# Attention with eight of sixteen softmax groups shifted and summed inside the exponential, and the output projection issued behind the next transposes

## The reference, cut to what matters

```python
x = x + _L0_conv_ref(_ln_c(x), rpb_table, w_qkv, w_proj, b_proj)
# inside: 7x7 windows (49 tokens), 4 heads of 32 channels
qkv  = (win @ w_qkv.T)                      # win: (2048, 49, 128)
attn = einsum('bhid,bhjd->bhij', q * scale, k) + bias + mask
attn = softmax(attn, axis=-1)
out  = einsum('bhij,bhjd->bihd', attn, v)
out  = out @ w_proj.T + b_proj
```

## Time and profile before

| What | us |
|---|---|
| median of 3 executions (8311.66 to 8319.39) | 8317.02 |
| the profiled execution's own time | 8316.43 |
| its span, first to last instruction | 8314.5 |
| attention stage, from the start to the last residual | 0 to about 1838 |
| one attention step in the steady part | 6.95 |

### The profile page before, as it was taken

The page is one execution under the profiler, slowest core; times in us unless marked ns, Lnnn a source line. Parts: engine busy times, 40 slices in busy tenths (PEclk is TensorE's granted clock), DMA queues, the critical chain, the costliest instruction groups (busy, mean ns, idle before and its releaser), DMA issues. The chain is left out here.

```text
span 8314.5 us, 428968 instructions
## 1 busy us (share of the span) xinstructions
PE 7686.1 (92%) x164847; PEld 4672.0 (56%) x164847; DVE 6157.6 (74%) x20999; ACT 4825.9 (58%) x15717; POOL 5973.0 (72%) x7343
## 2 busy tenths in 40 slices
PE   7999999978999999988979999979999799999999
PEld 6777777764444444436753333327777555555555
DVE  7999999979999999988856777758888322222222
ACT  4666666655566565558975555536666444444444
POOL 7888888868888888878966666637777444444444
PEclk9999999999999999999999999989999899999999
DMA  1222222222333333317885666658988122222222
GB/s 51 58 57 59 58 57 58 58 59 79 100 107 107 101 108 107 101 59 245 305 266 149 161 165 163 164 136 226 236 228 224 53 58 58 58 58 58 58 58 53
DMA packets 836450, 948.54 MB, mean 114 GB/s; under 512 B 329994, under 2 KB 701067, under 8 KB 812812
## 3 DMA queue, kind: packets, MB, share of 16 engines
q1 hardware_dynamic: 835404, 942.12, 40.4%
q10 hardware_dynamic: 576, 1.84, 0.1%
HBM read 574.02 MB, written 445.22 MB: 123 GB/s over the span
## 5 line engine op out<-in xcount | busy, mean ns | idle before, releaser
L988 PE MATMUL moe_pe_out<-moe_we,moe_xnT 128*128 128x512 f32 x3136 | 1474.9, 604 | 150.8 <-DVE moe_acc L882 143.6
L2329 ACT ACTIVATE rec_yT<-rec_ph 128x16 f32<-128x16 f32 x6272 | 871.9, 184 | 944.1 <-PE rec_ph L2462 939.8
L784 ACT ACTIVATE moe_scaled<-moe_pe_out,moe_gate 128x128 f32<-128x128 f32 x3136 | 894.4, 368 | 652.5 <-PE moe_pe_out L988 650.5
L2462 PEld LDWEIGHTS rec_ph<-rec_yT,rec_vt 128*32 128x32 f32 x50160 | 792.7, 108 | 690.3 <-ACT rec_yT L2329 585.1
L2462 PE MATMUL rec_ph<-rec_yT,rec_vt 128*32 128x16 f32 x50160 | 1087.6, 192 | 16.4 <-issue 6.3
L988 PEld LDWEIGHTS moe_pe_out<-moe_we,moe_xnT 128*128 128x128 f32 x3136 | 543.1, 190 | 912.2 <-issue 911.1
L2376 DVE COPY rec_xT<-rec_pin 128x512 f32<-128x512 f32 x196 | 135.6, 692 | 1212.9 <-PE rec_pin L2423 1212.9
L1622 PE MATMUL conv_p<-conv_c,conv_toep 32*32 32x432 f32 (+3 forms) x20480 | 960.8, 532 | 9.2 <-DVE conv_out L1587 4.7
L307 POOL TENSOR_SCALAR att_xn<-att_xin,att_mv,att_rstd 128x128 f32<-128x128 f32 x1024 | 868.1, 858 | 54.1 <-POOL att_rstd L303 54.1
L722 POOL TENSOR_TENSOR moe_paired<-moe_scaled 128x256 f32<-128x256 f32 x784 | 583.4, 744 | 162.3 <-ACT moe_scaled L784 123.0
L2304 POOL TENSOR_SCALAR rec_xn<-rec_xin,rec_mv,rec_rstd 128x127 f32<-128x127 f32 x784 | 634.7, 823 | 41.5 <-POOL rec_rstd L2301 41.5
(11 more groups left out here) (210 smaller groups left out, 19679.7 us busy)
## 6 DMA issues: line engine op xcount, KB each, us to landing
c<-foc_cs SPq DMA_DIRECT2D x128, 448.0 KB, 7.9
conv_cin<-c SPq DMA_DIRECT2D x64, 896.0 KB, 7.2
att_xin<-x_windows SPq DMA_DIRECT2D x512, 98.0 KB
moe_xin<-x SPq DMA_DIRECT2D x112, 448.0 KB, 6.4
x<-moe_acc SPq DMA_DIRECT2D x112, 448.0 KB, 2.8
foc_xin<-x SPq DMA_DIRECT2D x32, 1568.0 KB, 8.2
q<-foc_qs SPq DMA_DIRECT2D x32, 1568.0 KB, 8.4
ctx_all<-conv_out SPq DMA_DIRECT2D x128, 392.0 KB
```

The costliest lines, as they stand in the source:

```text
L784: ins = act.activation(scaled[:, b, e, :], pe_out[:, b, 1, e * C:(e + 1) * C], ACT.Identity, scale=g)
L988: pe.matmul(pe_out[:, b, half, :], xnT[:, n.slot(2), t, :], we[:, half * 4:half * 4 + 4, :].rearrange("d e c -> d (e c)"), start=True, sto ...
L2329: act.activation(yT[:, a, column(t, half)], ph[:, a, half, sums(t)], ACT.Sigmoid).then_inc(moved[half], 1)
L2462: ins = pe.matmul(ph[r:r + 32, n.slot(2), half, sums(t)], vt[:, r:r + 32], before, start=False, stop=True, skip_group_check=True)
```

## The change

Two things change in `attention_stage`.

First, the 16 groups are split at `SHIFTED = 8`. Groups 0 to 7 go the old way: DVE subtracts the maximum, ACT takes the exponential of all eight in one instruction, DVE sums them. For groups 8 to 15 ACT does it all: one instruction per group computes exp(x - max) with the negative maximum as a bias operand of one number per partition, and gives the group's sum as an accumulated output. So that it can be a bias, the maximum is now stored negated, and DVE's shift adds it. The eight single instructions come ahead of the joint one; they wait for the maximum, the joint one for the shift.

Second, PE issues `project` of the step before behind the next `turn`, not ahead of it. For that the call moves into the next turn of the loop (as `project(n-2)`), and so does `residual` on DVE.

```diff
+    SHIFTED = 8
-        mx = S.sb("mx", [P, PAIRS * HEADS])
+        negmax = S.sb("negmax", [P, PAIRS * HEADS])
             def exp(n):
+                act.wait_ge(maxed, n.val(1, 1))
+                for g in range(SHIFTED, PAIRS * HEADS):
+                    act.activation(pr[:, g, 0:WTOK], sc[:, g, 0:WTOK], ACT.Exp, bias=negmax[:, g:g + 1],
+                                   accum_out=sm[:, g:g + 1])
                 act.wait_ge(shifted, n.val(1, 1))
-                act.activation(pr[:, :, 0:WTOK], sc[:, :, 0:WTOK], ACT.Exp).then_inc(exped, 1)
+                act.activation(pr[:, 0:SHIFTED, 0:WTOK], sc[:, 0:SHIFTED, 0:WTOK], ACT.Exp).then_inc(exped, 1)
-                dve.tensor_reduce(mx[:], sc[:, :, 0:WTOK], AX.X, ALU.max).then_inc(maxed, 1)
+                dve.tensor_reduce(negmax[:], sc[:, :, 0:WTOK], AX.X, ALU.max, negate=True).then_inc(maxed, 1)
-                dve.tensor_tensor(sc[:, :, 0:WTOK], sc[:, :, 0:WTOK],
-                                  mx[:].unsqueeze(2).to_broadcast([P, HEADS * PAIRS, WTOK]),
-                                  ALU.subtract).then_inc(shifted, 1)
+                dve.tensor_tensor(sc[:, 0:SHIFTED, 0:WTOK], sc[:, 0:SHIFTED, 0:WTOK],
+                                  negmax[:, 0:SHIFTED].unsqueeze(2).to_broadcast([P, SHIFTED, WTOK]),
+                                  ALU.add).then_inc(shifted, 1)
-                dve.tensor_reduce(sm[:], pr[:, :, 0:WTOK], AX.X, ALU.add).then_inc(summed, 1)
+                dve.tensor_reduce(sm[:, 0:SHIFTED], pr[:, 0:SHIFTED, 0:WTOK], AX.X, ALU.add).then_inc(summed, 1)
...
+                if first >= 2:
+                    residual(n - 2, first - 2)
                 softmax_front(n, int(kind))
...
                 if last < -1:
                     turn(n + 1, 1)
+                if first >= 2:
+                    project(n - 2)
                 scores(n, first)
...
-                if first >= 1:
+                if last == -1:
                     project(n - 1)
```

More of the change, by code:

```diff
@@ L454, in step @@
                 softmax_back(n)
-                if first >= 1:
+                if last == -1:
                     residual(n - 1, first - 1)
-                if last == -1:
                     residual(n, first)
```

## The result

The changed kernel takes 8683.89 us (median of 4, 8675.73 to 8690.83), the kernel before 8317.22 us beside it. The ratio is 1.044, with a 95% interval from 1.0427 to 1.0454: slower by 367 us. The profiled execution took 8675.7 us. Nearly the whole loss lies in the attention stage: its last residual starts at 2194.30 us where it started at 1837.29, 357.0 us later, and the span is 359.3 us longer.

What follows compares the result with a forecast made beforehand. DVE's 6.95 us a step was taken as the bound, over a 6.56 us ring ACT, PE, ACT. After: 5.25 + 3.23 = 8.48 us, +1.53 over 253 steps = +387 on 8316.4, so 8704 us; range 8475 to 8840.

Steps and rivals of the forecast that it cites:

- the ring: Attention step's chain ACT, PE, ACT from exponentials to exponentials: 6.56 us before, forecast 8.48 us after.
- the clock: TensorE's clock in the attention stage: stays at full level; the rival of a fall, over 9400 us, had chance 0.04.
- The bound: Attention stage before the change: DVE's own work, 6.95 us a step, sets the step.
- The ring without the exponentials: Attention step's chain through PE, exponentials left out: 5.25 us after the projection's move takes out 0.43.
- the row of the stage's end: Profile step without token transposes at the attention stage's end: projection to scores 1.09 us, used for the moved projection.
- d: Distance from one single exponential to the next on ACT: 0.335 us, low end 0.23, high 0.42.
- The step: Attention step after the change: 8.48 us against 6.95, +1.53 us over 253 steps, +387 us.
- A: Rival on the single exponentials: sum is free, d = 0.23, +175 us, about 8491 us; chance 0.26.
- B: Rival on the single exponentials: dearer still, d = 0.42 or more, +559 us, 8875 us; chance 0.12.
- C: Rival on the attention step: faster than before if d is below 0.143; 8238 us at d = 0.105; chance 0.04.
- E: Rival: sums still hold DVE back, 6.1 us a step; chance 0.04 shared with outcomes between A and C.
- the second branch: Attention step through DVE's sum, inverse and product: 4.4 us in DVE's own ring, less than 5.25 through PE.

Runs made afterwards that it cites:

- The move alone: Changed kernel with no single exponentials (SHIFTED = 16), projection still behind the next transposes: 8316.75 us, ratio 1.0011 to the kernel before.
- without the sum: Changed kernel, but the eight single exponentials give no sum and VectorE sums all 16 groups: 8519.05 us, ratio 1.0246.
- plain singles: Changed kernel, but the eight single exponentials have neither bias operand nor sum; VectorE shifts and sums all 16 groups: 8438.18 us, ratio 1.0142.
- The fillers: Changed kernel with unread matmuls between token transposes and projection: four of 128x128, 8707.71 us; or two of 384 columns, 9418.76 us.
- the first run of two singles: Changed kernel with SHIFTED = 14, two single exponentials instead of eight: 8300.19 us (12 executions), ratio 0.998 to the kernel before.
- the second: The same program with SHIFTED = 14, two single exponentials, run again: 8327.69 us (12 executions), ratio 0.998 to the kernel before.

## Why the prediction was right

The forecast was 8704 us; measured are 8684, well inside the range of 8475 to 8840. The mechanism was the forecast one. The sum had two errors of opposite sign, -68 us in the ring and +35 us from the clock; that one takes back half of the other is luck.

- The bound. Right: VectorE at 6.95 us over a ring just beneath. The move alone changed nothing.
- The ring without the exponentials, 5.25 us forecast, 5.13 measured. The probability transposes to the query matmul took 0.93 us and not 1.03, the rest was right to 0.02 us. Projection to scores is 1.09 us, exactly the row of the stage's end.
- The single exponential, d = 0.335 forecast, 0.319 measured (2.55 / 8). Its parts were 0.14, 0.09 and 0.105, and are 0.135, 0.091 and 0.093. The sum had no row of its own; the nearest row, two neighbours of 7 columns 0.105 us apart, was close, and the accumulator read is a short instruction like these (0.19 us). The Trainium skill's rule for VectorE in "VectorE: DVE Perf Modes", section "Two Vector instructions with no wait between them", that an operation which also writes its accumulator is two instructions, is what ScalarE's rows show too: a second row of 0.19 us behind each single. The estimate of 0.228 us for a single with a bias operand from the figures of the Trainium skill ("ScalarE: Activation LUTs", "What ACT_TABLE_LOAD costs") stands beside 0.226 measured without the sum.
- The step, 8.48 forecast, 8.21 measured, which is 68 us less over 253 steps. With the clock's 35 us the sum is 8704 - 68 + 35 = 8671, against the profiled 8675.7.
- The clock. Here the prediction failed in part: it said that at 78% busy the clock would not fall, and gave that 0.04. It fell in one step of twelve, for 35 us. The error was to conclude from the one fall of the earlier trace rows, behind 3.30 of 6 us busy, that a busier PE has none; in the kernel after PE was busy for 82% of the time and the clock fell. With 0.43 and 0.75 us of idleness in one piece (plain singles, no sum) the clock held, with 1.5 it fell in one step of twelve, with 2.0 in nine of ten. PE was also busy for more of the time in the runs that held (93 and 89%, against 82 and 79%), and the runs don't tell the two apart. The fillers show that work in the gap ends the falls. The price in the forecast, over 9400 us, was for a clock that stays low, which did not happen.
- Rivals. A, the sum for nothing, is out by the 0.093 us that separate the singles with it from those without. B is out by d. C, faster, needed d under 0.143, and d was 0.319. The plain singles had 0.135 and were still slower, but they do not test C: VectorE carries the whole shift and sum there, so that neither the step nor the ring is the one that C was worked out for. E is out by DVE's waits.

The prediction had also timed the second branch, through VectorE's sum, inverse and product to the probability transposes, and found no wait there. That was right: the product runs from 1007.87 to 1008.85 and the transposes start at 1009.24, so there were 0.4 us of room. It was the expectations of the runs without the sum and with plain singles that took the ring of 5.13 or 5.42 us as given while they made this branch longer.

## What to carry to other kernels

Ask what stands behind the engine that you load, not only how busy it is: ScalarE was busy for 312 of 500 us before, so it had room for 2.6 us more a step, and the nine exponentials add only 3.08 - 0.88 = 2.20 us. Yet all 2.20 us lengthened the ring, because the projection's input was queued behind them; the step grew by less, 1.26 us, since the ring had 0.39 us of slack and lost 0.43 us by the move of the projection and 0.12 elsewhere. Moving work off the bound pays at most the distance to the next ring, here 0.39 us a step, or 0.82 with the projection moved, so move no more than that: three groups cost nothing here, eight cost 367 us. And splitting one wide instruction into narrow ones costs the fixed part each time; price it from neighbours of the same engine, one part for the instruction, one for each pointer operand, one for an accumulated output.

## What the runs showed of the hardware that I had not expected

- TensorE's granted clock fell although PE never idled for more than 1.5 us in one piece: in 21 steps of some 250 of 8.21 us, mostly 92 or 51 us apart. With 2.0 us in a step of 8.64 it fell in nine of ten.
- VectorE and POOL slow each other where their instructions overlap: POOL's addition takes 234 ns or 836, VectorE's product 977 or 1241. The same shift of 392 columns takes between 568 and 1495 ns in the kernel after, with 712 as the median; it lies off the path there. This is read from overlapping rows; no run took one of the two away.
- One program had two rhythms, 6.75 and 7.03 us a step, the longer one with that overlap in it. The kernel before has an upper level as well (3 of 23 executions at 8355 to 8361 us beside the first run of two singles, 1 of 23 at 8356 beside the second, 2 of 15 at 8355 and 8358 beside the move alone, which itself had 3 of 11 at 8354 to 8359), of which no profile was caught; that it has the same cause is a guess and not shown.
- Two `matmul` calls more in PE's loop of one stage went with a loss of over 700 us in later stages and seven times the traffic on the instruction queue; four shorter calls in the same place went with nine stops of 4.5 to 4.9 us in the loop itself and none later.
